# Eight taps of the first image's 5x5 convolution on four tiles, as TensorE products with diagonal matrices, with new orders of the first, second and last steps

## What is computed

```python
# attention block, on the channel-normalised image
qkv = conv2d(x, qkv_w)                                   # 1x1, 256 -> 768 channels
agg = conv2d(qkv, agg_dw_w, groups=dw_groups, padding=2) # 5x5 per channel: 25 taps
agg = conv2d(agg, agg_pw_w, groups=pw_groups)            # 1x1 in groups of 8
ms = jnp.concatenate([qkv, agg], axis=1)
q, k = relu(t[..., :DIM]), relu(t[..., DIM:2 * DIM])     # heads of 8, v with a column of ones
kv = jnp.einsum('bhnd,bhne->bhde', k, v)
out = jnp.einsum('bhnd,bhde->bhne', q, kv)
out = out[..., :-1] / (out[..., -1:] + EPS_ATT)
out = conv2d(out, proj_w)                                # then a batch norm, and x is added
# expert block, on the token-normalised image t
h = gelu(einsum('bsd,edf->ebsf', t, W1) + b1)            # 6 experts, 256 -> 341
out_e = einsum('ebsf,efd->ebsd', h, W2) + b2
t + einsum('be,ebsd->bsd', expert_weights, out_e)        # weights from a router over 11 patterns
```

## Time and profile before

| | us |
|---|---|
| median of three runs | 1521.37 (1518.8 to 1521.37) |
| the profiled execution | 1521.73 |
| its span, first to last instruction | 1520.0 |
| TensorE busy | 1322.4 |
| VectorE busy | 1274.4 |
| ScalarE busy | 1056.5 |
| GpSimd busy | 985.6 |

### The profile page before, as it was taken

One profiled execution on the slowest core, in us unless ns is written; L12 is line 12 of the kernel. 1 busy time (PEld: TensorE's weight loads), 2 busy tenths in 40 slices (PEclk: granted clock), 3 DMA queues, 4 the chain that ended last, 5 costly groups with the idle time before them and its releaser, 6 DMA issues.

```text
span 1520.0 us, 18453 instructions
## 1 busy us (share of the span) xinstructions
PE 1322.4 (87%) x6716; PEld 757.3 (50%) x6716; DVE 1274.4 (84%) x1305; ACT 1056.5 (70%) x1855; POOL 985.6 (65%) x744
## 2 busy tenths in 40 slices
PE   5423468799999999999999999999999998999897
PEld 3123345554565556555565556555555556555443
DVE  3899999999999989998999989998999999950000
ACT  3444356587678876878778777878687866764776
POOL 3575365576597668767678659766765756545644
PEclk7757689899999999999999999999999999999999
DMA  5200000001001000020001100100001000100000
GB/s 196 83 1 28 0 28 1 0 2 42 1 0 43 28 15 1 1 69 15 0 1 43 42 1 1 42 1 15 1 1 42 15 1 1 43 14 1 15 14 14
DMA packets 14250, 32.73 MB, mean 22 GB/s; under 512 B 2384, under 2 KB 5328, under 8 KB 13904
## 3 DMA queue, kind: packets, MB, share of 16 engines
...
## 4 chain that ended last, share of the span: by engine, by line
PE 70%; DVE 11%; ACT 9%; POOL 6%; issue 4%; DMA 1%; POOLq 0%; SPq 0%; ACTq 0%
PE wbk L488 26%; PE acc L501 20%; DVE dacc L1064 9%; PE wbk L580 7%; PE wbk L554 3%; PE wbk L539 3%; PE wbk L590 3%; PE wbk L534 2%; PE wbk L566 2%; PE wbk L573 1%; ACT kt L757 1%; POOL gl L911 1%; POOL dwo L881 1%; ACT sum_b L764 1%; ACT hb L685 1%
## 5 line engine op out<-in xcount | busy, mean ns | idle before, releaser
L1064 DVE SCALAR_TENSOR_TENSOR dacc<-qkvs,dww,dacc 128x930 f32<-128x930 f32 (+4 forms) x954 | 1053.1, 1187 | 0.0
L911 POOL TENSOR_TENSOR gl<-hb,gh 128x512 f16<-128x512 f32 x256 | 300.4, 1179 | 247.6 <-ACT hb L685 246.7
L881 POOL TENSOR_TENSOR dwo<-dwo,tapb 128x992 f32<-128x992 f32 (+1 forms) x104 | 241.4, 2321 | 51.6 <-ACT tapb L659 47.4
L779 ACT ACTIVATE hb<-wbk,b1s 128x512 f32<-128x512 f32 x256 | 174.4, 682 | 112.7 <-PE wbk L488 97.3
L501 PE MATMUL acc<-gh,w2h 128*128 128x512 f16 x512 | 195.3, 381 | 5.2 <-POOL gl L911 5.2
L501 PE MATMUL acc<-gl,w2h 128*128 128x512 f16 x512 | 195.2, 381 | 0.0
L501 PE MATMUL acc<-gh,w2l 128*128 128x512 f16 x512 | 195.0, 381 | 0.0
L684 ACT ACTIVATE gh<-hb,ewg 128x512 f16<-128x512 f32 x256 | 183.1, 715 | 0.7
L685 ACT ACTIVATE hb<-hb,ewg 128x512 f32<-128x512 f32 x256 | 182.4, 712 | 0.0
L488 PE MATMUL wbk<-th,w1h 128*128 128x512 f16 x512 | 153.1, 381 | 8.9 <-ACT kt L744 8.3
L488 PE MATMUL wbk<-tl,w1h 128*128 128x512 f16 x512 | 152.8, 380 | 0.0
(11 more groups left out here) (144 smaller groups left out, 2175.3 us busy)
## 6 DMA issues: line engine op xcount, KB each, us to landing
...
```

What stands on the lines that cost most here:

```text
L779: last = nc.scalar.activation(hb[:, f % GB, :], b[:], ACT.Gelu, bias=b1s[:, f % FT:f % FT + 1], scale=1.0 / (X_SCALE * W_SCALE))
L881: ins = nc.gpsimd.tensor_tensor(d3[:, oy, ox], d3[:, oy, ox], t3[:, iy, ix], ALU.add)
L911: nc.gpsimd.tensor_tensor(gl[:, f % GB, :], hb[:, f % GB, :], gh[:, f % GB, :], ALU.subtract).then_inc(g_low, 1)
L1064: ins = nc.vector.scalar_tensor_tensor(out=dst[:, oy, ox], in0=i3[:, jy, jx], scalar=dww[:, m, tap:tap + 1], in1=a3[:, oy, ox], op0=ALU.mu ...
```

## The change

Eight taps (`DIAG_TAPS`) of image 0's tiles 4, 5, 0, 1 become matrix products: ScalarE makes, for each tile and tap, a diagonal matrix of that tap's weights (piece `matrices`, eight 128x128 activations of the identity), TensorE multiplies it with the shifted half tile and sums the eight taps in one `wbk` bank (piece `diag`, one for each half tile, all in f32), and ScalarE copies the bank to `dwo`. The base of these tiles is four other taps instead of six, all of them added by GpSimd on top of that copy, so a base add of such a tile also waits until its `diag` is drained. VectorE keeps 14 instructions for each of these tiles, where it had 20. Tiles 2 and 3 of image 0 and all later images are computed as before.

The matrices lie in memory that is free at that time, two tiles' in `yrs[1]` and two tiles' in `hb`, so the load of image 1 into `yrs[1]` now waits until `diag` of tile 5 is done, and the load of image 0 into `yrs[0]` is issued behind that of `xa`.

The hand-made start becomes a string `FIRST`, and steps 1, 7 and 8 get strings of their own (`SECOND`, `LAST`, `END`). `PLAN`, now for steps 2 to 6, is reordered too. The places of VectorE's small tasks now depend on the image (`AGG_PLACES`, `RAW_PLACES`).

```diff
+DIAG_TAPS = [CENTER + TAPS, CENTER - TAPS, CENTER - 1, CENTER + 2 * TAPS, CENTER - 2 * TAPS, CENTER - 2,
+             CENTER + TAPS - 1, CENTER - TAPS - 1]
+DIAG_BASE = [CENTER + 2 * TAPS - 1, CENTER - 2 * TAPS - 1, CENTER + 2 * TAPS - 2, CENTER - 2 * TAPS - 2]
+DIAG_TILES = (4, 5, 0, 1)
 def base_taps(s, m):
-    return (0 if m in (2, 3) else len(BASE_TAPS)) if s == 0 else 3
+    if s == 0:
+        return DIAG_BASE if m in DIAG_TILES else []
+    return BASE_TAPS[:3]
...
-    for j in range(1, B + 1):
-        for word in PLAN:
+    for j in range(B + 1):
+        plan = FIRST if j == 0 else SECOND if j == 1 else END if j == B else LAST if j == B - 1 else PLAN
+        for word in plan:
...
+FIRST = """
+squares.0.0.0 squares.0.0.1 sums.0.0 weights.0 stats.0.0 rnorm.0.0 rbc.0.0.0 rbc.0.0.1 weights.1 apply.0.0.0
+apply.0.0.1 high.0.0.0 low.0.0.0 high.0.0.1 low.0.0.1 qkv.0.2.0 qkv.0.2.1 qkv.0.3.0 qkv.0.3.1 qkv.0.4.0
+matrices.0.4 qkv.0.4.1 qkv.0.5.0 qkv.0.5.1 b squares.1.0.0 squares.1.0.1 diag.0.4.0 matrices.0.5 diag.0.4.1
+sums.1.0 b matrices.0.0 diag.0.5.0 diag.0.5.1 matrices.0.1 qkv.0.0.0 b qkv.0.0.1 qkv.0.1.0 b b qkv.0.1.1
+stats.1.0 rnorm.1.0 b diag.0.0.0 b rbc.1.0.0 b rbc.1.0.1 diag.0.0.1 apply.1.0.0 apply.1.0.1 b b b high.1.0.0
+b diag.0.1.0 diag.0.1.1 low.1.0.0 high.1.0.1 b tok.0.0 tok.0.1 low.1.0.1 tok.0.2 tok.0.3 tok.0.4 b tok.0.5 b
+tok.0.6 tok.0.7 relu_q.0.0 b kv.0.0.0 kv.0.0.1 mask.0.0 relu_q.0.1 att.0.0.0 att.0.0.1 att.0.0.2 b att.0.0.3
+scale.0.0.0 att.0.0.4 att.0.0.5 att.0.0.6 att.0.0.7 scale.0.0.1 back.0.0.0.0 back.0.0.0.1 back.0.0.1.0
+back.0.0.1.1 agg.0.2.0 agg.0.2.1 agg.0.3.0 agg.0.3.1 qkv.1.2.0 qkv.1.2.1 qkv.1.3.0 qkv.1.3.1 b squares.2.0.0
+squares.2.0.1 sums.2.0 b stats.2.0 b b rnorm.2.0 b b agg.0.4.0 rbc.2.0.0 rbc.2.0.1 apply.2.0.0 apply.2.0.1
+agg.0.4.1 agg.0.5.0 agg.0.5.1 qkv.1.4.0 b qkv.1.4.1 qkv.1.5.0 qkv.1.5.1 kv.0.1.0 b b b kv.0.1.1 b mask.0.1
+""".split()
+SECOND = """
...
+rbc.-1.1.1 apply.-1.1.0 F att.0.0.3 scale.0.0.0 G G att.0.0.4 apply.-1.1.1 att.0.0.5 att.0.0.6 att.0.0.7
+high.-1.1.0 high.-1.1.1 qkv.1.2.0 qkv.1.2.1 scale.0.0.1 qkv.1.3.0 low.-1.1.0 low.-1.1.1 logits.-1
+back.0.0.0.0 back.0.0.0.1 back.0.0.1.0 back.0.0.1.1 G qkv.1.3.1 agg.0.2.0 S F exp.-1 agg.0.2.1 agg.0.3.0
...
+LAST = """
...
+rnorm.-1.1 G relu_q.0.1 rbc.-1.1.0 G rbc.-1.1.1 apply.-1.1.0 apply.-1.1.1 F att.0.0.0 att.0.0.1 att.0.0.2 b
+att.0.0.3 scale.0.0.0 G att.0.0.4 att.0.0.5 att.0.0.6 b att.0.0.7 high.-1.1.0 high.-1.1.1 low.-1.1.0
+scale.0.0.1 S F back.0.0.0.0 low.-1.1.1 S G F logits.-1 back.0.0.0.1 F back.0.0.1.0 back.0.0.1.1 S G F
...
+END = """
...
+squares.-1.1.0 F squares.-1.1.1 sums.-1.1 S S F stats.-1.1 rnorm.-1.1 G S rbc.-1.1.0 rbc.-1.1.1 F
+apply.-1.1.0 apply.-1.1.1 high.-1.1.0 high.-1.1.1 low.-1.1.0 low.-1.1.1 S G G logits.-1 F S F S G F exp.-1 S
...
+AGG_PLACES = {1: (20, 24, 76, 81), 2: (17, 25, 78, 87), 7: (20, 23, 75, 84), 8: (19, 21, 75, 83)}
+RAW_PLACES = {0: (89, 90), 1: (64, 68), 2: (66, 72), 7: (69, 74)}
...
-            sp.wait_ge(weights_ready, 1)
-            for i in range(2):
-                sp.dma_start(yrs[i][:], x[i].rearrange("(k p) n -> p k n", p=P)).then_inc(yr_loaded, 16)
...
+                elif it == ("matrices", 0, 4):
+                    sp.wait_ge(weights_ready, 1)
+                    sp.dma_start(yrs[0][:], x[0].rearrange("(k p) n -> p k n", p=P)).then_inc(yr_loaded, 16)
+                elif it == ("diag", 0, 5, NCH - 1):
+                    sp.wait_ge(bank_filled, FILL[it] + 1)
+                    sp.dma_start(yrs[1][:], x[1].rearrange("(k p) n -> p k n", p=P)).then_inc(yr_loaded, 16)
...
+                elif what == "diag":
+                    m, c = it[2:]
+                    if c == 0:
+                        pe.wait_ge(matrices_made, (DIAG_TILES.index(m) + 1) * len(DIAG_TAPS))
+                        pe.wait_ge(bank_drained, drained(("qkv", s, m, NCH - 1)))
...
+                    for i, tap in enumerate(order):
+                        (oy, ox), (iy, ix) = half(tap, c)
+                        last = nc.tensor.matmul(b3[:, oy, ox], diag_matrix(m, DIAG_TAPS.index(tap)), i3[:, iy, ix],
+                                                start=(i == 0), stop=(i == len(order) - 1))
...
+                if what == "matrices":
+                    m = it[2]
+                    act.wait_ge(weights_ready, 1)
+                    for i, tap in enumerate(DIAG_TAPS):
+                        nc.scalar.activation(diag_matrix(m, i), ident[:], ACT.Copy, scale=dww[:, m, tap:tap + 1]
+                                             ).then_inc(matrices_made, 1)
+                    continue
...
+                elif what == "diag":
+                    m, c = it[2:]
+                    last = nc.scalar.activation(dwo[:, m, c * CH:(c + 1) * CH], b[:], ACT.Copy)
...
+                        if i == 0:
+                            pool.wait_ge(bank_drained, drained(("diag", s, m, NCH - 1)))
```

More of the change, by code:

```diff
@@ L90, in schedule, with give @@
     finished = [0]
[L92 to L97, removed]
+    def give(it):
+        o.append(it)
+        given.add(it)
     def base(n):
@@ L101, in base @@
         del waiting[:n]
-    def rest():
-        base(len(waiting))
     def add_base(s, a):
-        waiting.extend(("base", s, m, i) for m in (a, a + 1) for i in range(base_taps(s, m)))
+        waiting.extend(("base", s, m, i) for m in (a, a + 1) for i in range(len(base_taps(s, m))))
     def second():
@@ L209, in schedule @@
         first()
-    rest()
     return o
-PLAN = """
[L215 to L223, removed]
-squares.2.0.0 squares.2.0.1 S sums.2.0 agg.0.3.1 b F S G G S b stats.2.0 rnorm.2.0 F G G F S S F G G S S b
@@ L225 @@
-rbc.2.0.0 F S b G F S F rbc.2.0.1 agg.0.4.0 apply.2.0.0 agg.0.4.1 G F G F S b agg.0.5.0 b agg.0.5.1 S G S G
-F qkv.1.4.0 G apply.2.0.1 F G S kv.0.1.0 F S F F F G F S G S qkv.1.4.1 G qkv.1.5.0 b qkv.1.5.1 G S F F S G b
-F S b G G kv.0.1.1 mask.0.1 S S F b S G b
-""".split()
-BANKED = ("qkv", "agg", "kv", "stats", "rbc", "att", "back", "proj", "tok", "logits", "ffn")
+FIRST = """
+squares.0.0.0 squares.0.0.1 sums.0.0 weights.0 stats.0.0 rnorm.0.0 rbc.0.0.0 rbc.0.0.1 weights.1 apply.0.0.0
+apply.0.0.1 high.0.0.0 low.0.0.0 high.0.0.1 low.0.0.1 qkv.0.2.0 qkv.0.2.1 qkv.0.3.0 qkv.0.3.1 qkv.0.4.0
@@ new lines @@
+G G F b qkv.1.4.0 apply.2.0.1 F G S G kv.0.1.0 S F F G F S F G S qkv.1.4.1 G b qkv.1.5.0 F qkv.1.5.1 G F F S
+S G b G kv.0.1.1 b S G S F b G mask.0.1 S S b
+""".split()
+PLAN = """
+S agg.-1.0.0 F agg.-1.0.1 agg.-1.1.0 agg.-1.1.1 S G att.-1.1.0 att.-1.1.1 att.-1.1.2 G att.-1.1.3 F G
+qkv.0.0.0 qkv.0.0.1 b scale.-1.1.0 att.-1.1.4 S att.-1.1.5 att.-1.1.6 att.-1.1.7 b scale.-1.1.1 qkv.0.1.0
+qkv.0.1.1 high.1.0.0 F back.-1.1.0.0 G S b F low.1.0.0 F S back.-1.1.0.1 back.-1.1.1.0 S back.-1.1.1.1 G F
@@ new lines @@
+high.1.0.1 G proj.-1.0.0 tok.0.0 b S proj.-1.0.1 proj.-1.1.0 tok.0.1 tok.0.2 tok.0.3 tok.0.4 tok.0.5 tok.0.6
+low.1.0.1 b G proj.-1.1.1 tok.0.7 relu_q.0.0 F squares.-1.1.0 kv.0.0.0 squares.-1.1.1 sums.-1.1 b kv.0.0.1
+mask.0.0 F relu_q.0.1 stats.-1.1 rnorm.-1.1 G att.0.0.0 att.0.0.1 S att.0.0.2 att.0.0.3 b rbc.-1.1.0
+rbc.-1.1.1 apply.-1.1.0 F F apply.-1.1.1 scale.0.0.0 att.0.0.4 G att.0.0.5 att.0.0.6 G S att.0.0.7 qkv.1.2.0
+scale.0.0.1 high.-1.1.0 qkv.1.2.1 high.-1.1.1 qkv.1.3.0 S low.-1.1.0 low.-1.1.1 logits.-1 back.0.0.0.0
@@ L230 @@
+S G F F G S F S G F G F G F S G S G F S G F S G S F S G S G F S G F G S S G G S S G S F F S
+""".split()
+AGG_PLACES = {1: (20, 24, 76, 81), 2: (17, 25, 78, 87), 7: (20, 23, 75, 84), 8: (19, 21, 75, 83)}
+RAW_PLACES = {0: (89, 90), 1: (64, 68), 2: (66, 72), 7: (69, 74)}
+BANKED = ("diag", "qkv", "agg", "kv", "stats", "rbc", "att", "back", "proj", "tok", "logits", "ffn")
 ORDER = schedule()
@@ L415, in clip, with half @@
             return (slice(oy, oy + ny), slice(ox, ox + nx)), (slice(iy, iy + ny), slice(ix, ix + nx))
+        def half(tap, c):
+            (oy, ox), (iy, ix) = clip(tap)
+            rows = HH // NCH
+            lo, hi = max(oy.start, c * rows), min(oy.stop, (c + 1) * rows)
+            return (slice(lo - c * rows, hi - c * rows), ox), (slice(iy.start + lo - oy.start, iy.start + hi - oy.start), ix)
         @block.sync
```

135 lines of the change are left out of this document (62 added, 73 removed).

## The result

| | before | after |
|---|---|---|
| median | 1521.37 us | 1497.8 us (1496.57 to 1499.0) |
| ratio of the runs | | 0.9844, interval 0.9824 to 0.9865 |
| span of the profiled execution | 1520.0 | 1495.0 |
| TensorE busy | 1322.4 | 1365.2 |
| VectorE busy | 1274.4 | 1256.3 |

What follows compares the result with a forecast made beforehand. It took VectorE as the full engine in the ramp and TensorE as setting the pace in middle steps. From 1521.7 us it took 16 (ramp), 5 (step 7), 1 (step 8) and 3 (steps 2 to 6): 1497, range 1479 to 1514.

Steps and rivals of the forecast that it cites:

- The ramp: Start of the kernel: VectorE keeps 12 us of its gain, TensorE's waits give 4, together 16 us, between 6 and 26.
- The products: TensorE in the ramp: 64 f32 products of 0.86 us, 52 us in all at 2.4 GHz, loads put at nothing.
- Rivals 3 and 4: Ramp: products run at 1.2 GHz, 1541 us, 7%; or their loads don't overlap, 1513 us, 8%.
- rival 4: Ramp: loads of the diagonals don't overlap, 24 us more on TensorE, 1513 us in all; chance 8%.
- The diagonals: ScalarE in image 0: 32 diagonals of 128 columns at 0.28 us each, 2.2 us a tile, 9 in all.
- The sums are ready in time: Image 0: GpSimd's sums at 112 (tile 5) and about 142 (tile 1), VectorE at 113 and 142.5; 0 to 5 us allowed.
- VectorE loses 26 us and stands for 14 at image 1: Ramp: 24 fewer VectorE instructions save 26 us; image 1's late base makes it wait some 14, so it keeps 12.
- Rival 1: Whole gain arrives: image 1's base comes at once, ramp gives 26 us, orders 5 + 5 + 5, 1481 us; chance 18%.
- Steps 2 to 6: Middle steps: new order gains 0.6 us a step, 3 us in all, between -10 and 10; the widest unknown.
- Step 7: TensorE's wait on `scale`, before `back`: 3 us for the wait and 2 for the clock, 5 us gained, between 0 and 6.
- step 8: Last step: END puts expert work between `rbc` and `logits`, 1 us gained, between -2 and 5.
- Rival 2: Orders give the gain back: 2 us more in each of steps 2 to 6, 1519 us, no change; chance 10%.

Runs made afterwards that it cites:

- diag_twice: The changed kernel with every diagonal product made twice, the second eight overwriting the first: 1546.2 us.
- fewer_adds: The changed kernel without base taps 2 and 3 of image 1's tiles 2 and 3 (four scalings, four GpSimd adds): 1491.0 us.
- base_first: The changed kernel with image 1's six base pieces right behind the qkv of tiles 2 and 3, and image 2's norm moved later in FIRST: 1491.6 us.
- mid_old: The changed kernel with the old PLAN and its old places in steps 2 to 6 alone: 1507.5 us.
- last_old: The changed kernel with the old PLAN and places in step 7 alone, END kept: 1491.9 us.

## Why the prediction was right, and where it was not

The time was forecast as 1497 and came out as 1497.8, but this agreement is partly luck: errors in the ramp, in the middle, in the last steps and at the start cancel.

**The ramp: mechanism right, 16 forecast, 16 to 18 measured.** Step by step in the trace of the changed kernel:

- The products. Forecast: 52 us, 0.41 for an instruction, at full clock, loads hidden. The trace has the first two tiles in one piece of 26.25 us for 64 instructions, and the granted clock from 54 to 112 is 1.00. Rivals 3 and 4 fall with this line. Its loads take 0.19 us each and stand in no gap. That the 0.41 us don't hide a load in series is seen at the f32 products of 128 columns at 92.44: they follow one another at 0.111 us (1.78 us for 16), less than their own load of 0.20 us. By these two rows an instruction costs 0.83 ns for each further column and next to nothing beside (an estimate). So the rule of the Trainium skill that made rival 4 ("TensorE: Matmul & The Clock Gate", section "What overlaps and what doesn't") doesn't hold for these products.

```profile
59.86 26.25 PE L561 MATMUL wbk<-qkvs,yr 128*128 128x512 f32 x64
...
92.44 1.95 PE L627 MATMUL wbk<-mean_w,rb 128*128 128x128 f32 x16
...
96.00 6.69 PE L561 MATMUL wbk<-qkvs,hb 128*128 128x512 f32 x16
...
104.90 19.83 PE L561 MATMUL wbk<-qkvs,hb 128*128 128x512 f32 x48 [0.87 <-ACT rb L818]
```

- The diagonals. Forecast: 2.2 us a tile on ScalarE. Measured: 2.43.
- The sums are ready in time. Forecast: tile 5 at 112, tile 1 at 142, hardly any slack. GpSimd's last adds end at 108.3 and 138.7, VectorE comes at 109.1 and 141.6 and doesn't wait; diag_twice puts the slack at 5 us.

```profile
104.44 3.82 POOL L933 TENSOR_TENSOR dwo<-dwo,tapb 128x900 f32<-128x900 f32 x2 [2.76 <-ACT tapb L704]
...
136.88 1.81 POOL L933 TENSOR_TENSOR dwo<-dwo,tapb 128x900 f32<-128x900 f32 x1 [0.52 <-ACT tapb L704]
...
109.13 5.83 DVE L1112 SCALAR_TENSOR_TENSOR dacc<-qkvs,dww,dwo 128x1024 f32<-128x1024 f32 x2
...
141.55 2.75 DVE L1112 SCALAR_TENSOR_TENSOR dacc<-qkvs,dww,dwo 128x1024 f32<-128x1024 f32 x2
```

- VectorE loses 26 us and stands for 14 at image 1. Measured: image 0 ends at 172.6, and the two waits at 182.0 and 190.3 are 9.5 + 7.0 = 16.5 us. Rival 1, by which the whole gain arrives, falls with them: image 1's plain taps begin at 193.5 instead of 206.7, 13 us earlier, where 12 were forecast. fewer_adds and base_first show that this wait costs most of its time, and base_first that half of it comes from the norm of image 2 among the adds.
- The first `ffn` near 280: it is at 277.2, before at 297.0.
- What I didn't see: the products and the order of step 1 need each other. I had put 12 us to the products' account and 4 to the order's; alone they bring 6 and 4, and 10 is less than the 16 to 18 of both.

**Steps 2 to 6: the term that was mis-sized.** I took 0.6 us a step, 3 in all, and called it the widest unknown. It was 2.1 in a full middle step, 9.3 in all, so a step of 163.9 us and not of 165 to 166, and mid_old shows that it is the order's alone. TensorE's idle time in a step went from 6.7 us to 5.3.

**Step 7: the step that failed.** I wrote that LAST puts a `second` and an `ffn` right before `back` and forecast 5 us of gain. That wait did go. But I read the new order only around the wait that I knew, and not what had been moved for it, the `rbc` ahead of `att`. Steps 7 and 8 together cost 4.7 us instead of giving 6, and last_old puts most of this on step 7. In step 8 `logits` waits for 3.72 us exactly as before, so the forecast gain of 1 us there didn't come either.

In sum: 16 + 3 + 5 + 1 = 25 forecast; in the two profiles 18 + 9 - 5 measured, and 2 us of a start that varies by itself. Rival 2 put a loss into steps 2 to 6; those got shorter, and the loss came in step 7.

One reading in the prediction was off and changed nothing: in rows 1 TensorE is at nine tenths from the ninth slice on, from about 304 us, not from the tenth.
